# A two-layer image kernel: depthwise taps moved from TensorE to VectorE, half of one layer's statistics to ScalarE

## The chip, the cores and the metric

The kernel runs on one core of one Trainium2 chip, in one launch for the whole batch. The time is the device time of that core in microseconds (us). A core has these engines: TensorE (PE in the profile, with its weight loads as PEld) for matrix products, VectorE (DVE), ScalarE (ACT), GpSimd (POOL), and SyncE (SP), which here issues all transfers. Each engine works through its own instruction stream in order, and they meet at semaphores.

## The reference

Eight images of 128 channels and 64 x 64 pixels pass two layers. What is computed, cut to its core:

```
# layer 0
ll, lh, hl, hh = haar(x)                       # 4 bands of 32 x 32
q, k, v = conv1x1(ll, qkv_w)                   # 8 heads of 16, 1024 tokens
attn = l2norm(q) @ l2norm(k).T * 0.25          # keep the 512 largest of each row
ll_out = group_norm(conv1x1(softmax(top_half(attn)) @ v, proj_w))
y = depthwise_3x3(concat(lh, hl, hh), dw_w)    # 384 channels, 9 taps
y = group_norm(conv1x1(silu(group_norm(y)), pw_w))
x = x + 0.1 * inverse_haar(ll + ll_out, bands + alpha * y)
y = gelu(group_norm(conv1x1(x, w1)))           # 128 -> 256 channels
x = x + 0.1 * group_norm(conv1x1(y, w2))
# layer 1
q, k, v = 16, 16 and 128 channels of x, 4096 tokens
x = gamma * conv1x1(softmax(q @ k.T / 4) @ v, Wo) + x
```

A group norm needs the mean and variance of each group over all pixels before its scale is known.

## The kernel before

The images go through a pipeline of two kinds of stretches. `slots(b)` runs the attention of image b's layer 0 and, interleaved with it, that of image b - 1's layer 1. `between(f, n)` lies between two such stretches: it finishes layer 0 of image f (projection, group norms, feed-forward layers, planes of q, k and v for layer 1) and opens image n (bands, depthwise convolution, pointwise products, q, k, v of layer 0). The program is between, slots for image 0 alone, seven times between and slots for two images, and between and slots for the last image's layer 1. Six of the seven are one loop body.

Within each stretch every engine has a list written out by hand, one call per piece of work. A call waits for its semaphores and issues its instructions, so the order of the calls is the order on the engine. In `slots`, `search(h)` is the list for one of seven steps per image: the top-half threshold of head h, the row maxima of the next chunk of layer 1 (`maxima`, matmul into one PSUM bank and reduction from it), the masked weights of the previous head (`half_m`), and the norm of a chunk.

The pieces of `between` that matter here, with the lines of their instructions:

- `taps(k, t)` on DVE: tap t of the depthwise convolution of block k of 128 channels, a multiply (L2451) or multiply-add (L2454) of 128 x 1024 into `Y`. The padded bands `PAD` come from POOL. Blocks 1 and 2 have nine taps each here.
- `conv(0, h, row)` on PE (L1090): block 0, as matmuls with diagonal weights (`diag`), nine per half of the image, into PSUM; ACT copies the halves to `Y`. Each float32 matmul is two PE instructions in the profile.
- `conv(k, h)` on DVE (L2467): statistics of a half block. `moments`, `variance`, `scales` (L2335 to L2362) are the small steps of a group norm, with a sum over groups on PE (L968), a power on POOL (L2625) and a spreading on PE (L979).
- `heads_out`, `proj`, `add0` (L2318, L955, L2324, L2370): product of the heads, projection and its statistics, and the four additions that make `X1`, the input of the feed-forward layer. `squares` on PE (L1050) sums the squares of q and k; `clamp` and `norms` on DVE (from L2408) follow it, `spread` on PE (L1079) and `normal` on DVE (L2429) apply the result.
- `ffn1(k)`, k = 0 to 15: matmul (PE, L990) into one of four PSUM banks, eviction (ACT, L1479) and BN_STATS (DVE, L2377). PE may be three evictions ahead. Then `gelu` (ACT, L1487), `ffn2` (L1000, L1493, L2384), `points` (pointwise products, L1105, L2477, L1584), `norm2` and `add2` (L1500, L2392), and `values1` (L1023, L1522).

## Time and profile before

| | before |
|---|---|
| median of 3 runs | 5553.13 us (5548.35 to 5555.53) |
| the profiled execution's own time | 5553.66 us |
| its span, first to last instruction | 5551.9 us |
| mean granted TensorE clock | 0.917 |
| PE, DVE, ACT, POOL busy | 86, 83, 77, 5% |
| longest part of the chain that ended last | DVE 37%, PE 31%, issue 19%, ACT 7% |

Busy time is the time in which an engine has an instruction at work. The chain that ended last is followed back from the last instruction, at each step to what released it. A row of a timeline has the start, the time, engine, line, operation, output and input, the number of instructions merged into it and, in brackets, how long the engine had waited and for what. The granted clock is TensorE's: 1.0 is 2.4 GHz and 0.5 is 1.2 GHz.

### The profile page before, as it was taken

Reading aid. Unit: us, or ns where it says so; the run is one execution under the profiler, and the core shown is the slowest. Engines: PE = TensorE matmul, PEld = TensorE weight load, DVE = VectorE, ACT = ScalarE, POOL = GpSimd, SP = SyncE. Lnnn points to the kernel's source line nnn. Section 1 sums busy time; section 2 is a strip of 40 time slices with the busy share of each in tenths; the row PEclk is TensorE's granted clock in tenths of the full one; section 3 lists DMA queues with packets and bytes.
Section 4 is the critical chain, followed back from the end, with each engine's and each line's share of the span. In section 5 each row is a group of like instructions: output and inputs, shape, how many; then the busy total and the mean of one; then the engine's idle time right before and its main releaser. Section 6 shows DMA issues by size and latency. Waiting matters only on the chain.

```text
span 5551.9 us, 93420 instructions
## 1 busy us (share of the span) xinstructions
PE 4778.7 (86%) x30180; PEld 3098.8 (56%) x30180; DVE 4622.0 (83%) x9087; ACT 4261.9 (77%) x6779; POOL 261.5 (5%) x125
## 2 busy tenths in 40 slices
PE   4444899988999889988999889998899989997899
PEld 2000366654666456664666546665566636665588
DVE  4887789987999789987899879998799979996553
ACT  3884699948998599966999589984999769995333
POOL 2001000020000200010000100002000100000000
PEclk7555899998999989998999989999899989998899
DMA  1001200012001110012000120011200120001100
GB/s 58 8 10 52 62 15 16 13 60 64 16 21 44 38 53 18 16 61 63 15 16 13 60 64 16 17 47 35 55 16 18 55 69 15 16 13 44 35 12 16
DMA packets 103270, 185.34 MB, mean 33 GB/s; under 512 B 48536, under 2 KB 53560, under 8 KB 98008
## 3 DMA queue, kind: packets, MB, share of 16 engines
q1 hardware_dynamic: 102744, 178.93, 10.5%
q8 instruction: 256, 4.19, 0.3%
q14 instruction: 270, 2.21, 0.1%
HBM read 107.99 MB, written 67.37 MB: 32 GB/s over the span
## 4 chain that ended last, share of the span: by engine, by line
DVE 37%; PE 31%; issue 19%; ACT 7%; SPq 2%; DMA 1%; POOL 1%; DVEq 1%; ACTq 0%; POOLq 0%
PE PS L621 12%; DVE M L1798 8%; DVE MX L1966 7%; DVE work L1789 5%; PE PS L587 4%; PE PS L561 3%; ACT work L1216 3%; DVE work L1781 3%; DVE arena L1895 3%; PE PS L605 3%; PE PS L551 2%; PE PS L483 2%; ACT work L1271 1%; PE PS L1090 1%; PE PS L633 1%
## 5 line engine op out<-in xcount | busy, mean ns | idle before, releaser
L621 PEld LDWEIGHTS PS<-V,work 128*128 128x128 f32 x16384 | 2112.1, 193 | 164.6 <-ACT work L1281 23.1
L621 PE MATMUL PS<-V,work 128*128 128x129 f32 x16384 | 2130.1, 277 | 13.7 <-ACT work L1281 12.4
L1216 ACT ACTIVATE work<-arena,T 128x1024 bf16<-128x1024 f32 x1504 | 1714.9, 1145 | 23.4 <-DVE T L1709 13.1
L1966 DVE TENSOR_REDUCE MX<-PS 128x1 f32<-128x512 f32 x2048 | 1394.9, 686 | 249.9 <-PE PS L587 235.4
L1281 ACT ACTIVATE work<-PS 128x1024 f32<-128x1024 f32 x1024 | 1041.6, 1019 | 319.1 <-PE PS L605 317.2
L587 PE MATMUL PS<-KP,QP 96*128 96x512 bf16 x2048 | 844.0, 413 | 71.7 <-DVE MX L1966 32.8
L1798 DVE MAX8 M<-work 128x8 f32<-128x512 f32 x1024 | 651.2, 680 | 0.5
L605 PE MATMUL PS<-QP,KP 99*128 99x512 bf16 x2048 | 624.0, 387 | 23.2 <-ACT work L1281 19.8
L1208 ACT ACTIVATE arena<-PS 128x1024 f32<-128x1024 f32 x512 | 524.0, 1023 | 147.0 <-PE PS L483 138.5
L1895 DVE SCALAR_TENSOR_TENSOR arena<-PS,work 128x512 f32<-128x512 f32 x896 | 600.9, 683 | 33.7 <-ACT work L1271 24.3
L1271 ACT ACTIVATE work<-PS 128x512 f32<-128x512 f32 x896 | 513.8, 591 | 116.0 <-PE PS L551 112.8
L587 PEld LDWEIGHTS PS<-KP,QP 96*128 96x128 bf16 x2048 | 200.7, 98 | 502.2 <-DVE MX L1966 411.8
L483 PE MATMUL PS<-work 96*128 96x512 bf16 x1024 | 349.5, 427 | 98.5 <-ACT arena L1208 98.5
L551 PE MATMUL PS<-work 99*128 99x512 bf16 x896 | 332.5, 384 | 80.4 <-DVE arena L1895 60.4
L1781 DVE TENSOR_SCALAR work<-arena,T 128x1024 f32<-128x1024 f32 x512 | 371.4, 747 | 4.4 <-DMA scrL<-work 2.7
L1789 DVE TENSOR_SCALAR work<-work,FL 128x1024 uint32<-128x1024 uint32 x512 | 374.2, 744 | 1.0
L561 PE MATMUL PS<-arena,VT 128*17 128x256 f32 x4096 | 345.4, 415 | 3.4 <-DVE arena L1887 3.3
L1216 ACT ACTIVATION_READ_ACCUMULATOR work<-arena,T 128x1 f32 x1504 | 295.4, 196 | 0.0
L605 PEld LDWEIGHTS PS<-QP,KP 99*128 99x128 bf16 x2048 | 182.0, 99 | 185.4 <-ACT work L1281 81.2
L483 PEld LDWEIGHTS PS<-work 96*128 96x128 bf16 x1024 | 80.0, 102 | 263.6 <-ACT arena L1208 171.4
L551 PEld LDWEIGHTS PS<-work 99*128 99x128 bf16 x896 | 83.1, 98 | 198.7 <-DVE arena L1895 164.1
L2645 POOL TENSOR_TENSOR work<-work 128x1024 f32<-128x1024 f32 x8 | 22.6, 2826 | 3494.1 <-DMA work<-in_x 3494.1
(193 smaller groups left out, 4157.7 us busy)
## 6 DMA issues: line engine op xcount, KB each, us to landing
work<-scr SPq DMA_DIRECT2D x752, 32.0 KB, 1.8
work<-in_x SPq DMA_DIRECT2D x16, 1024.0 KB, 7.4
arena<-in_x SPq DMA_DIRECT2D x8, 2048.0 KB, 11.2
scrX<-arena SPq DMA_DIRECT2D x8, 2048.0 KB, 6.4
XR<-scrX SPq DMA_DIRECT2D x64, 256.0 KB, 2.7
out<-YO SPq DMA_DIRECT2D x64, 256.0 KB, 2.0
scr<-work SPq DMA_DIRECT2D x24, 512.0 KB, 2.7
scrL<-work SPq DMA_DIRECT2D x24, 512.0 KB, 7.9
```

Of the source, the lines that this page charges most:

```text
L483: last = mm(PS[:, c, :], qp(h)[0:KS, 128 * i:128 * i + 128], kp(h)[0:KS, 512 * c:512 * c + 512], start=True, stop=True)
L587: mm(PS[:, maxbank(c, k, l0), :], QP1[0:KS, c * 512 + 128 * i:c * 512 + 128 * i + 128], KP1[0:KS, 512 * w:512 * w + 512], start=True, stop ...
L605: last = mm(PS[:, pairbanks(k, l0) + t, :], KP1[0:KA, 128 * mt:128 * mt + 128], QP1[0:KA, j * 512:j * 512 + 512], start=True, stop=True)
L621: last = mm(PS[:, 5 + i // 2, 136 * (i % 2):136 * (i % 2) + 129], P1[:, (16 * j + k) % 3, t, 128 * i:128 * i + 128], V1[:, mt, :], start=( ...
L1216: A(junk[:, m % 2, :], scores(h, i), ACT.Sign, scale=-1.0, bias=T[:, h % 2, i:i + 1], accum_out=CA[:, h % 2, i:i + 1]).then_inc(s["ca"], 1)
L1271: A(JA[:, mt % 2, 512 * c:512 * c + 512], PS[:, c, :], ACT.Exp, scale=0.25).then_inc(s["e" if c else "eh"], 1)
L1281: A(P1[:, (16 * j + k) % 3, :, :].rearrange("p t n -> p (t n)"), PS[:, u:u + 2, :].rearrange("p a n -> p (a n)"), ACT.Exp, scale=0.25).the ...
L1781: cp.did(V.tensor_scalar(JD[:, c, :], scores(h, i), T[:, h % 2, i:i + 1], None, ALU.subtract))
L1789: cp.did(V.tensor_scalar(JDu[:, c, :], JDu[:, c, :], FL[:, h % 2, i:i + 1].bitcast(u32), None, ALU.bitwise_xor))
L1798: cp.did(V.max(M8[:, i, a, :], JD[:, c, 512 * a:512 * a + 512]))
L1895: V.scalar_tensor_tensor(scores(h, mt)[:, 512 * c:512 * c + 512], PS[:, c, :], 0.0, JA[:, mt % 2, 512 * c:512 * c + 512], ALU.is_ge, ALU.m ...
L1966: V.reduce_max(MX[:, c % 2, i, w:w + 1], PS[:, maxbank(c, k, l0), :], AX.X).then_inc(s["mr"], 1)
```

## The change

The convolution on PE goes: `NPE`, `diag` and the POOL instruction that filled it, `conv` on PE and the copies of it on ACT. DVE does all 27 taps. In exchange the statistics of the first eight of ffn1's sixteen pieces leave DVE: ACT sums each piece while it evicts it (`accum_out` into `FS`), and two new instructions `power1(o)` square 2048 columns each and sum them into `FQ`; their output goes to `V1`, which `values1` overwrites later. `moments(3)` puts the sums together. All lists are written anew, those between images most, and those of the search, the opening and the closing as well.

```diff
-NPE = 1
-        diag = sb("diag", [128, 9 * NPE, 128])
+        FS, FQ = sb("FS", [128, 8]), sb("FQ", [128, 2])
...
@@ ACT, between @@
-                    A(HF[:, o, 512 * ch:512 * ch + 512], PS[:, k % 4, :], ACT.Copy).then_inc(s["hc"], 1)
+                    A(HF[:, o, 512 * ch:512 * ch + 512], PS[:, k % 4, :], ACT.Copy, **({} if o else {"accum_out": FS[:, ch:ch + 1]})).then_inc(s["hc"], 1)
+
+                def power1(o):
+                    if not fin:
+                        return
+                    act.wait_ge(s["hc"], f * 16 + 4 * o + 4)
+                    act.wait_ge(s["pv1"], f * 128 + 3)
+                    A(V1[:, 16 * o:16 * o + 16, 0:128], HF[:, 0, 2 * N0 * o:2 * N0 * o + 2 * N0].rearrange("p (a c) -> p a c", c=128), ACT.Square, accum_out=FQ[:, o:o + 1])\
+                        .then_inc(s["fq"], 1)
...
+                    if k == 0:
+                        act.wait_ge(s["fq"], (f + 1) * 2)
...
-                def conv(k, h):
-                    if not opn:
-                        return
-                    if k == 0 and h == 0:
-                        act.wait_ge(s["pad"], (n + 1) * 3)
-                    act.wait_ge(s["cv"], n * (2 * NPE) + 2 * k + h + 1)
-                    act.wait_ge(s["bc"], n * 6 + 2 * k + h + 1)
-                    A(Y[:, k, 512 * h:512 * h + 512], PS[:, 5 + h, :], ACT.Copy).then_inc(s["ye"], 1)
...
+                power1(0)
                 ffn1(10)
...
                 ffn1(15)
-                values0(1)
+                power1(1)
                 gelu(0)
...
@@ DVE, moments @@
-                    w = {0: 2, 1: 2, 2: 2, 3: 8, 4: 8}[g]
+                    if g == 3:
+                        dve.wait_ge(s["fq"], (f + 1) * 2)
+                        dve.wait_ge(s["hc"], f * 16 + 8)
+                        ch.link(V.tensor_reduce(N.mv[:, 0, 0:1], FS[:, :], AX.X, ALU.add))
+                        ch.link(V.tensor_tensor(N.mv[:, 0, 1:2], FQ[:, 0:1], FQ[:, 1:2], ALU.add))
+                        ch.wait(mark["bn"])
+                        ch.link(V.bn_aggr(N.mv[:, 1, :], N.bn[:, 8:16, :].rearrange("p a s -> p (a s)")))
+                        ch.link(V.tensor_scalar(N.st[:, 0, :], N.mv[:, 0, :], 1.0 / N1, None, ALU.mult))
+                        ch.link(V.tensor_tensor(N.st[:, 1, 1:2], N.mv[:, 1, 0:1], N.mv[:, 1, 0:1], ALU.mult))
+                        ch.link(V.tensor_tensor(N.st[:, 1, 1:2], N.st[:, 1, 1:2], N.mv[:, 1, 1:2], ALU.add))
+                        V.tensor_copy(N.st[:, 1, 0:1], N.mv[:, 1, 0:1]).then_inc(s[N.sem + "1"], 1)
+                        return
+                    w = {0: 2, 1: 2, 2: 2, 4: 8}[g]
...
-                    V.bn_stats(BH[:, 2 * k + h, :], PS[:, 5 + h, :] if k < NPE else Y[:, k, 512 * h:512 * h + 512]).then_inc(s["bc"], 1)
+                    V.bn_stats(BH[:, 2 * k + h, :], Y[:, k, 512 * h:512 * h + 512]).then_inc(s["bc"], 1)
...
@@ DVE, list of between @@
+                taps(0, 0)
                 taps(2, 0)
-                taps(1, 0)
                 taps(2, 1)
```

What the lists make of the order is seen at three places. The first is DVE at the front of a stretch between two images: L2451 and L2454 (L2435 and L2438 after) are the taps, L2318 (L2290) is the product of the heads, BN_STATS of `BN<-PS` the projection's statistics. Before:

```order
L2451 TENSOR_SCALAR work<-PAD,w_dw 128x1024 x2
L2454 SCALAR_TENSOR_TENSOR work<-PAD,w_dw,work 128x1024 x4
L2317 REGISTER_ALU
L2318 TENSOR_TENSOR arena<-arena 128x1024
L2454 SCALAR_TENSOR_TENSOR work<-PAD,w_dw,work 128x1024
L2323 ISA
L2324 BN_STATS BN<-PS 128x6
```

The same place in the changed kernel:

```order
L2435 TENSOR_SCALAR work<-PAD,w_dw 128x1024 x2
L2438 SCALAR_TENSOR_TENSOR work<-PAD,w_dw,work 128x1024 x4
L2435 TENSOR_SCALAR work<-PAD,w_dw 128x1024
L2289 REGISTER_ALU
L2290 TENSOR_TENSOR arena<-arena 128x1024
L2438 SCALAR_TENSOR_TENSOR work<-PAD,w_dw,work 128x1024 x3
L2295 ISA
L2296 BN_STATS BN<-PS 128x6
```

One tap more stands ahead of the product, and three instead of one stand between it and the statistics.

The second is PE around ffn1 (L990, L987 after). L1050 (L1047) are the squares, L1090 the convolution. Before:

```order
L979 MATMUL PS<-GG,indT 128x2
L1046 REGISTER_ALU
L1050 MATMUL PS<-cons,work 128x8 x16
L1090 MATMUL PS<-PAD,diag 128x512 x3
L990 MATMUL PS<-arena,w 128x512 x4
```

After, there, and behind it the end of ffn1 with the spreads (L1076), the group sum (L965) and its spreading (L976):

```order
L976 MATMUL PS<-GG,indT 128x2
L1043 REGISTER_ALU
L1047 MATMUL PS<-cons,work 128x8 x16
L987 MATMUL PS<-arena,w 128x512 x4
...
L1076 MATMUL PS<-cons,work 128x128 x4
L986 REGISTER_ALU
L987 MATMUL PS<-arena,w 128x512
L986 REGISTER_ALU
L987 MATMUL PS<-arena,w 128x512
L1076 MATMUL PS<-cons,work 128x128 x4
```

Ffn1 stands directly behind the squares now, and a spread stands ahead of its last two matmuls.

The third is DVE in a step of the search, behind the threshold: L1966 (L1938) are row maxima, L1739 (L1711) an update of the search, L1948 (L1920) `head_out`. Before:

```order
L1966 TENSOR_REDUCE MX<-PS 128x1
L1723 REGISTER_ALU
L1739 SCALAR_TENSOR_TENSOR T<-CA,T 128x4
L1965 REGISTER_ALU
L1966 TENSOR_REDUCE MX<-PS 128x1
L1965 REGISTER_ALU
L1966 TENSOR_REDUCE MX<-PS 128x1
L1948 COPY OT<-PS 128x256
```

After:

```order
L1938 TENSOR_REDUCE MX<-PS 128x1
L1695 REGISTER_ALU
L1711 SCALAR_TENSOR_TENSOR T<-CA,T 128x4
L1920 COPY OT<-PS 128x256
L1937 REGISTER_ALU
L1938 TENSOR_REDUCE MX<-PS 128x1
L1937 REGISTER_ALU
L1938 TENSOR_REDUCE MX<-PS 128x1
```

The copy of the head's output has moved ahead of two row maxima.

## Rows read from the trace of the kernel before

**Rows 1.** The page's first part, the whole span.

```profile
PE 4778.7 (86%) x30180; PEld 3098.8 (56%) x30180; DVE 4622.0 (83%) x9087; ACT 4261.9 (77%) x6779; POOL 261.5 (5%) x125
```

**Rows 2.** Windows: us, busy us of each engine, clock, DMA; stretch between images, search step.

```profile
1197.00:1307.50 110.50, 98.37 (x364) 52.27 (x364) 77.08 (x149) 67.43 (x98) 8.22 (x7) 0.95 0.16 40
...
1510.47:1573.70 63.23, 59.44 (x430) 41.45 (x429) 58.95 (x123) 59.15 (x99) 0.00 (x0) 1.00 0.06 17
```

**Rows 3.** Timeline of DVE, image 2, front of the stretch.

```profile
1200.24 1.42 DVE L2451 TENSOR_SCALAR work<-PAD,w_dw 128x1024 f32<-128x1024 f32 x2 [4.19 <-issue]
1201.57 4.99 DVE L2454 SCALAR_TENSOR_TENSOR work<-PAD,w_dw,work 128x1024 f32<-128x1024 f32 x4
1206.48 1.22 DVE L2318 TENSOR_TENSOR arena<-arena 128x1024 f32<-128x1024 f32 x1
...
1209.44 0.70 DVE L2324 BATCH_NORM_STATS2 BN<-PS 128x6 f32<-128x512 f32 x1 [0.55 <-PE PS L955]
...
1215.60 0.16 DVE L2362 TENSOR_TENSOR SH<-vecs,SM 128x1 f32<-128x1 f32 x1
...
1220.75 1.22 DVE L2370 TENSOR_TENSOR arena<-arena 128x1024 f32<-128x1024 f32 x1
```

**Rows 4.** Timeline of PE, image 2.

```profile
1215.11 4.70 PE L1050 MATMUL PS<-cons,work 128*128 128x8 f32 x32
1219.66 5.21 PE L1090 MATMUL PS<-PAD,diag 128*128 128x512 f32 x6
1224.71 8.75 PE L990 MATMUL PS<-arena,w 128*128 128x512 f32 x20
...
1266.69 10.57 PE L1105 MATMUL PS<-work,w_pw 128*128 128x512 f32 x24 [0.22 <-ACT work L1575]
```

**Rows 5.** Windows, image 2 (columns as above; granted clock third from last).

```profile
1215.00:1220.00 5.00, 5.00 (x35) 4.99 (x35) 4.53 (x7) 1.20 (x1) 0.00 (x0) 0.77 0.00 0
1220.00:1225.00 5.00, 5.00 (x7) 2.01 (x7) 4.66 (x14) 0.00 (x0) 0.00 (x0) 0.55 0.00 0
...
1245.00:1250.00 5.00, 3.96 (x17) 2.41 (x17) 3.82 (x7) 2.63 (x3) 1.09 (x1) 1.00 0.00 0
```

**Rows 6.** Timeline of PE, last image.

```profile
5101.72 15.83 PE L990 MATMUL PS<-arena,w 128*128 128x512 f32 x32 [6.54 <-DVE arena L2370]
...
5125.52 15.87 PE L1000 MATMUL PS<-arena,w 128*128 128x512 f32 x32 [3.05 <-ACT arena L1487]
```

**Rows 7.** Timeline of DVE, first image.

```profile
51.24 0.29 DVE L2408 TENSOR_SCALAR SSM<-PS 128x128 f32<-128x128 f32 x1 [5.97 <-PE PS L1050]
...
73.47 0.35 DVE L2335 BATCH_NORM_AGGREGATE MVH<-BH 128x2 f32<-128x12 f32 x3
```

**Rows 8.** Timeline of PE, first image, and the stretch that follows it.

```profile
81.98 13.46 PE L1105 MATMUL PS<-work,w_pw 128*128 128x512 f32 x24 [2.18 <-ACT work L1575]
...
594.61 5.43 PE L1090 MATMUL PS<-PAD,diag 128*128 128x512 f32 x6
```

**Rows 9.** Timeline of ACT, image 2.

```profile
1239.54 0.60 ACT L1479 ACTIVATE arena<-PS 128x512 f32<-128x512 f32 x1 [0.26 <-PE PS L990]
...
1247.37 4.64 ACT L1487 ACTIVATE arena<-arena,SH,SC 128x1024 f32<-128x1024 f32 x4 [5.44 <-DVE SH L2362]
...
1288.82 1.02 ACT L1208 ACTIVATE arena<-PS 128x1024 f32<-128x1024 f32 x1
1289.72 0.20 ACT L1208 ACTIVATION_READ_ACCUMULATOR arena<-PS 128x1 f32 x1
```

**Rows 10.** Timeline of DVE, image 2, moments of ffn1.

```profile
1241.99 0.60 DVE L2335 BATCH_NORM_AGGREGATE MV<-BN 128x2 f32<-128x48 f32 x2
...
1243.02 0.17 DVE L2339 COPY ST<-MV 128x2 f32<-128x2 f32 x1
```

**Rows 11.** Waits of DVE in the search step: us, times, longest.

```profile
DVE MX L1966 <- PE PS L587: 2.1, 6, 0.5
DVE TP L1878 <- issue: 1.2, 1, 1.2
```

502 lines of the change are left out of this document (234 added, 268 removed).

## The prediction

> **What bounds the kernel now.** Read the page first. PE, DVE and ACT are busy for 86, 83 and 77% of 5551.9 us [rows 1], so no engine alone bounds the whole. Busy time by stretch comes next: in one step of the search (63.23 us, seven such per image) DVE and ACT work 59 us and PE 59.4 us, and in one stretch between images (1197.0 to 1307.5) PE works 98.4 of 110.5 us while DVE works 77.1 and ACT 67.4 [rows 2]. The change adds work to the two engines with room in that stretch and takes 20 us of PE's busy time from it, some of it clocked low, so the question is which of the 98.4 us the end of the stretch waits for. The timelines of DVE, PE and ACT over the stretch answer that. The chain is: heads ready, projection, its statistics, four additions that make X1, the sixteen matmuls of the first feed-forward layer (ffn1), their statistics, gelu, ffn2, the pointwise products, normalization, key and value planes of layer 1. The convolution on PE is in that chain only where its matmuls stand in PE's queue ahead of something ready.
>
> **The change, part by part.** I follow image 2, the others repeat it within a few tenths of a us in the stretches I opened.
>
> *Front, up to X1.* DVE begins its taps at 1200.24, and two first taps take 1.42 us, four later ones 4.99, so 0.7 and 1.2 us each [rows 3]. Before, six taps precede the product of the heads at 1206.48, now seven: +0.7. Behind it stood one tap and then 0.55 us of idle time before the projection's statistics at 1209.44; now stand three taps (3.6 us): 1208.35 + 3.6 = 1211.95, some 2.5 us later than before. Then come two statistics (1.25), moments (0.75), a tap (1.2), variance (0.65), a tap (1.2) that covers PE and POOL, and the scales (0.65): 1217.65 instead of 1215.76 [rows 3], as PE's convolution no longer delays the spreading of the sums. With 1.35 on ACT and four additions of 1.17 the last X1 comes at 1223.7 instead of 1221.97 (1220.75 + 1.22). That is +1.75.
>
> *What the convolution cost there.* X1 was whole at 1221.97, but ffn1 began at 1224.71, because the second half of the convolution ran from 1219.66 for 5.21 us [rows 4]. It now begins at 1223.75: a gain of 0.95, no more.
>
> *The clock.* Those six instructions took 5.21 us, while six of the same shape take 2.64 at the rate of the pointwise products (24 in 10.57) [rows 4]. The granted clock tells why: 0.77 in 1215 to 1220 and 0.55 in 1220 to 1225, where 0.5 is 1.2 GHz and 1.0 is 2.4 GHz [rows 5]. It fell during the 32 narrow instructions of the squares and rose only during the convolution, so the convolution took the slow stretch upon itself and ffn1 ran at 2.4 GHz (20 instructions in 8.75 us, 0.43 each). Without it PE stands nearly idle from 1210 to 1217, runs the squares and idles some 2 us more. ffn1 then starts at 1.2 GHz. The last image, which has no convolution, shows the price: its 32 instructions of ffn1 take 15.83 us against 13.8 at 0.43 each, so 2.0 [rows 6]. The bounds are 0 (clock still high) and 2.9, from the first image's pointwise products: 24 instructions in 13.46 us against 10.57 in image 2 [rows 4, 8]. I take 2.0, from the same matmuls. In the Trainium skill, "TensorE: Matmul & The Clock Gate", sections on the clock gate and its oscillation, the low clock is the default, activity releases it, and a burst of matmuls behind an idle gap starts slow. By that rule the removed matmuls were useful as activity, which speaks against the change. The trace agrees, with 0.55 turning into 1.00 just as the convolution ends; without this effect the stretch would keep its old clock and the third rival below would hold.
>
> *Statistics on ACT.* Eight of sixteen BN_STATS leave DVE (0.6 us each, 4.9 us), nine taps come (10.2 us), so DVE gains 5.3 us of work. It has room until ffn1, as the taps fill the time in which it waited. ACT gets eight accumulator reads (0.2 us each; they fit the 0.26 us that it waits between evictions [rows 9]) and two Squares of 128 x 2048. No instruction of 2048 columns is in the trace. Gelu of 1024 columns takes 1.16 us (four in 4.64) and an eviction of 512 columns 0.60 [rows 9], so 2048 cost at most 2 x 1.16 = 2.3 and at least 1.16 + 0.84 = 2.0, if each further 512 columns cost the 0.42 by which an eviction of 1024 (1.02) exceeds one of 512 [rows 9]; with the read I take 2.3 (2.2 to 2.5). The first Square stands behind ffn1's tenth eviction, where the four PSUM buffers and one spread matmul group hide it. The second stands behind the sixteenth and has no cover, for moments(3) waits on it. From the last eviction's end to the finished moments it was 3.1 us (1240.1 to 1243.19, DVE beginning its moments at 1241.99 [rows 9, 10]). Now it is 2.3 for the Square and 1.5 for seven small DVE instructions (0.2 each): 3.8, so +0.7. Behind the waiting moments are queued normal(1), the taps and the scales of gelu.
>
> *PE's order.* spread(0) now stands ahead of the last two ffn1 matmul groups: +1.0. Sum to gelu: -0.95 + 2.0 + 1.0 + 0.7 = +2.75.
>
> *ffn2 and the pointwise products.* PE ran these back to back, and the products began at 1266.69 [rows 4]. In the gap between ffn1 and ffn2, which grows to about 11 us with two spreads in it, the clock falls: it did so even before, in image 1, where six convolution instructions at 594.61 took 5.43 us [rows 8], and the last image's ffn2 took 15.87 against 13.97, so 1.9 [rows 6]. Taking 1.9 (0 to 2.9), and 0 for group(1), whose moments DVE has near 1262 (gelu's scales at 1250, then five taps, six statistics, a product, moments: 12 us) while PE comes to it near 1263.5 (start 1253, four times 1.75, a spread, the slow start): the products start 4.65 late. DVE's new order takes moments(4) ahead of the products' second statistics, -1.0. One eviction now stands on ACT between the normalizations, which set the pace of the last additions, +0.5, and the one of points(2,0) inside ACT's full tail up to the value planes +0.3. Stretch: +4.4 us, seven times: +31.
>
> *First and last image.* At the start DVE sat idle 5.97 us until 51.24 for the squares [rows 7]. Eighteen taps now stand ahead of clamp, which comes at 55.1, and nine of 27 remain: the high bands' moments move from 73.5 [rows 7] to 76 (35.1 + 30.7 of taps + 3.9 for clamp and norms + 2.0 of products + 3.9 of statistics + 0.5 of waits), +2.5. In the last image no tap exists; the Squares cost 0.8 of lag, and 1.8 where DVE was nearly abreast: +2.6.
>
> *The lists of the search.* All lists are rewritten here too. A step has 3.3 us of DVE waits: 2.1 for PE's row maxima, in six places, and 1.2 for the register load [rows 11]. The maxima share one PSUM bank, so two in a row on DVE wait 0.4 to 0.5 for a round trip. The new order puts head_out ahead of maxima 15 (which waited 0.41) and two flips instead of one ahead of maxima 0 (0.39), but puts maxima 29 directly behind the tiny excess pair, and leaves 15/16 and 17/18 in pairs. Net -0.3 per step. Bounds: -2.1, all waits gone, and +1.0, which is five new back-to-back pairs less what they replace; PE and ACT have under 4 us of room each, so a delay on either shows. 49 steps at -0.3: -15. The opening without layer 1 and the closing steps I put at 0 (plus or minus 6).
>
> **Sum.** 31 + 2.5 + 2.6 - 15 = +21 on the profiled execution's 5553.66 (span 5551.9 and 1.8 around it): 5574.8. The median is 0.5 below that execution: 5574.
>
> **The rivals.** *The search lists win more.* If 0.9 us of the 2.1 goes per step, 49 x 0.9 = 44 against 36 of the rest: 5545, and at most 5487 if all waits go. For it: the waits named are short and each can be filled. Against: PE is as full as DVE (59.4 of 63.23), and a filled wait on one is paid on the other. *The search lists lose:* +0.5 per step, one more round trip: 36 + 25 = +61, 5614. For it: several maxima now follow each other closer (28, excess, 29; both halves of masks ahead of 25). Against: the order moves most pieces by one place only. *The clock holds.* If PE stays at 2.4 GHz at both starts, the stretch loses 3.9 and gets a stall of about 0.5 at group(1): +1.0 per image, 7 + 5 - 15 = -3: 5550. For it: in 1245 to 1250 of image 2 the clock was 1.00 although PE idled for a fifth [rows 5]; against it, the squares already brought it down. *No effect of the edit:* excluded, since 288 matmul instructions go and 72 taps come; but a sum near zero is the case just told. *A faster result through less PE work as such* would need the convolution's 20 us in the chain; only 2.7 us of it is there.
>
> **Chances.** Forecast 0.45, with its own range 5560 to 5590; search lists lose 0.17; clock holds 0.18; search lists win more 0.20. What repeats of this kernel can tell from no change is 0.2%, 11 us. Slower by more: nearly all of the first two, 0.60. Within: half of the clock case and the edges, 0.22. Faster: the better lists and a bit of the clock case, 0.18. The range that holds 8 of 10 runs from 5538 to 5606, leaving out the ends of both list cases.
>
> **What would show it.** In the new profile of an image: X1's last addition about 1.7 us later against the first tap; the first ffn1 matmuls at 0.85 us per instruction instead of 0.43 and a granted clock near 0.5 there; again at ffn2; a Square of 2.1 to 2.3 us directly ahead of moments(3), with DVE idle before it; gelu about 2.8 us and the pointwise products 4 to 5 us later; a stretch of 115 instead of 110.5 us; a step of the search at 62.9 instead of 63.2. The forecast is wrong if ffn1 starts at full clock, if the step differs by over 0.5 us from 63.2 either way, or if the first Square makes PE wait for PSUM.

## The result and the profile after

The changed kernel takes 5624.85 us (median of 4 runs, 5623.88 to 5635.42) against 5553.76 for the kernel before beside it: a ratio of 1.0132 with an interval of 1.0120 to 1.0145. It is slower, as forecast, but by 71 us where 21 were forecast, and outside the range. The page begins:

```profile
span 5622.1 us, 92914 instructions
...
PE 4734.7 (84%) x29892; PEld 3103.1 (55%) x29892; DVE 4679.0 (83%) x9111; ACT 4279.0 (76%) x6859; POOL 261.7 (5%) x124
```

TensorE is busy 44 us less than in [rows 1], VectorE 57 us more, and the span is 70.2 us longer, so busy time doesn't say where the loss is. I cut the span at marks on VectorE: the instruction that converts the number found (FOUNDI) marks a head of the search as found, 64 of them in all. Sums in us, from the two timelines:

| | before | changed | difference |
|---|---|---|---|
| start to first head found | 166.9 | 172.7 | +5.9 |
| image 0, the other heads | 338.0 | 335.3 | -2.7 |
| seven times: last head to the next image's first | 1500.7 | 1512.9 | +12.2 |
| 7 x 7 search steps | 3039.7 | 3091.8 | +52.1 |
| last head to the end | 506.6 | 509.3 | +2.7 |

The search steps, which the forecast had at -15, are three quarters of the loss. The stretch between images is the smaller part, but only in this table: from VectorE's first tap to the first row maxima it is 3.7 us longer in the mean, 26 us in seven images, while the way from the last head to the first tap is 1.5 us shorter and that from the first row maxima to the first head 0.5 us, 14 us in seven. Cut at VectorE's first tap, the end of X1, the first of gelu's scales and the first of the silus', image 2 reads before and after (windows: us, then busy us of PE, PEld, DVE, ACT and POOL, the granted clock, DMA share, GB/s):

```profile
1200.24:1221.97 21.73, 20.29 (x74) 11.82 (x73) 18.89 (x29) 5.45 (x9) 0.54 (x1) 0.89 0.02 6
1221.97:1246.94 24.97, 23.24 (x75) 11.95 (x74) 20.79 (x43) 11.32 (x18) 3.41 (x2) 0.95 0.00 1
1246.94:1262.14 15.20, 15.20 (x52) 7.44 (x52) 13.06 (x26) 13.56 (x17) 0.54 (x1) 1.00 0.00 0
```

```profile
1213.23:1238.25 25.02, 17.77 (x54) 11.96 (x54) 22.93 (x32) 6.49 (x10) 1.52 (x1) 0.57 0.02 6
1238.25:1264.02 25.77, 20.99 (x67) 11.31 (x68) 23.78 (x43) 15.29 (x30) 3.52 (x2) 0.83 0.00 0
1264.02:1279.68 15.66, 14.52 (x49) 7.88 (x49) 14.10 (x29) 11.78 (x13) 0.54 (x1) 0.80 0.01 1
```

In each part the clock is lower and VectorE fuller. Both could be the reason, and the experiments had to separate them. Now the search (the same view of the changed kernel: a step of image 2 that is nearly as long as in [rows 2], a long one, and 2 us pieces around the long one's beginning):

```profile
1388.16:1451.47 63.31, 59.30 (x430) 41.28 (x428) 58.76 (x121) 58.89 (x99) 0.00 (x0) 1.00 0.06 16
1514.84:1579.90 65.06, 60.74 (x430) 42.79 (x429) 59.15 (x123) 59.09 (x99) 0.00 (x0) 0.97 0.06 17
```

```profile
1516.00:1518.00 2.00, 0.86 (x6) 0.43 (x5) 1.70 (x7) 1.23 (x4) 0.00 (x0) 1.00 0.02 4
1518.00:1520.00 2.00, 1.65 (x11) 1.18 (x9) 1.45 (x3) 2.00 (x5) 0.00 (x0) 0.84 0.01 2
1520.00:1522.00 2.00, 2.00 (x10) 1.84 (x10) 0.69 (x1) 1.83 (x3) 0.00 (x0) 0.50 0.03 2
1522.00:1524.00 2.00, 2.00 (x14) 1.61 (x14) 0.69 (x1) 0.61 (x2) 0.00 (x0) 0.81 0.09 18
```

Before, the 42 steps between the first and seventh head of the seven images take 62.9 to 63.5 us. Now 23 take 64.4 to 65.1 and the others 63.1 to 63.5, and the seventh step of each image, in the closing list, went from 55.2 to 56.5. In 22 of the 23 the granted clock has one dip to 0.5 that lasts 3.4 us and begins 4 to 5 us behind the found head. In the kernel before no step has one. TensorE's timeline there (turn is L526, the row maxima L586, scores and weights of layer 1 L604 and L620):

```profile
1515.21 1.06 PE L620 MATMUL PS<-V,work 128*128 128x129 f32 x8
1517.00 0.23 PE L526 MATMUL PS<-identb,TP 128*24 128x128 bf16 x1 [0.74 <-DVE TP L1853]
1517.63 0.39 PE L586 MATMUL PS<-KP,QP 96*128 96x512 bf16 x1 [0.40 <-DVE MX L1938]
1517.85 0.60 PE L604 MATMUL PS<-QP,KP 99*128 99x512 bf16 x2
1518.80 0.39 PE L586 MATMUL PS<-KP,QP 96*128 96x512 bf16 x1 [0.35 <-DVE MX L1938]
1519.03 1.60 PE L620 MATMUL PS<-V,work 128*128 128x129 f32 x8
1520.43 0.63 PE L586 MATMUL PS<-KP,QP 96*128 96x512 bf16 x1
1520.85 1.93 PE L620 MATMUL PS<-V,work 128*128 128x129 f32 x8
```

Three short waits stand around the turn (0.74, 0.40, 0.35 us), then the eight instructions that took 1.06 us take 1.60 and 1.93. The waits alone don't tell which step gets a dip: in the step at 1388.16 above, which has none, they are 0.78, 0.40 and 0.35. The kernel before waits longer once (1.42 us for the turn) and has no dip:

```profile
1558.63 0.38 PE L587 MATMUL PS<-KP,QP 96*128 96x512 bf16 x1
1560.44 0.23 PE L527 MATMUL PS<-identb,TP 128*24 128x128 bf16 x1 [1.42 <-DVE TP L1881]
1560.60 0.61 PE L605 MATMUL PS<-QP,KP 99*128 99x512 bf16 x2
1561.06 0.39 PE L587 MATMUL PS<-KP,QP 96*128 96x512 bf16 x1
1561.29 1.06 PE L621 MATMUL PS<-V,work 128*128 128x129 f32 x8
```

### The profile page after: what moved, and what is told of

The parts are those of the page before. It is cut to its first block and busy times, and to the rows that moved or that the text cites. A ratio compares the mean times of both kernels' runs of the same rounds, so it can differ in the third digit from the quotient of the medians.

```text
span 5622.1 us, 92914 instructions
## 1 busy us (share of the span) xinstructions
PE 4734.7 (84%) x29892; PEld 3103.1 (55%) x29892; DVE 4679.0 (83%) x9111; ACT 4279.0 (76%) x6859; POOL 261.7 (5%) x124
## 5 line engine op out<-in xcount | busy, mean ns | idle before, releaser
L620 PEld LDWEIGHTS PS<-V,work 128*128 128x128 f32 x16384 | 2113.5, 194 | 168.2 <-issue 34.9
L620 PE MATMUL PS<-V,work 128*128 128x129 f32 x16384 | 2140.2, 278 | 5.2 <-ACT work L1255 3.9
L1938 DVE TENSOR_REDUCE MX<-PS 128x1 f32<-128x512 f32 x2048 | 1394.2, 685 | 259.5 <-PE PS L586 241.7
L586 PE MATMUL PS<-KP,QP 96*128 96x512 bf16 x2048 | 849.3, 416 | 122.6 <-DVE MX L1938 86.8
L604 PE MATMUL PS<-QP,KP 99*128 99x512 bf16 x2048 | 620.0, 384 | 39.2 <-ACT work L1255 32.9
L586 PEld LDWEIGHTS PS<-KP,QP 96*128 96x128 bf16 x2048 | 201.6, 98 | 557.4 <-DVE MX L1938 466.1
L550 PE MATMUL PS<-work 99*128 99x512 bf16 x896 | 319.7, 385 | 41.0 <-DVE arena L1867 32.6
L560 PE MATMUL PS<-arena,VT 128*17 128x256 f32 x4096 | 319.0, 411 | 1.1 <-DVE arena L1859 1.1
L1190 ACT ACTIVATION_READ_ACCUMULATOR work<-arena,T 128x1 f32 x1504 | 309.9, 206 | 0.0
L604 PEld LDWEIGHTS PS<-QP,KP 99*128 99x128 bf16 x2048 | 176.1, 98 | 204.5 <-ACT work L1255 113.9
L2438 DVE SCALAR_TENSOR_TENSOR work<-PAD,w_dw,work 128x1024 f32<-128x1024 f32 x192 | 250.8, 1345 | 3.1 <-DVE RN L2404 1.3
L2627 POOL TENSOR_TENSOR work<-work 128x1024 f32<-128x1024 f32 x8 | 22.6, 2828 | 3565.0 <-DMA work<-in_x 3565.0
## 6 DMA issues: line engine op xcount, KB each, us to landing
arena<-in_x SPq DMA_DIRECT2D x8, 2048.0 KB, 10.2
```

What stands on the lines that cost most here:

```text
L586: mm(PS[:, maxbank(c, k, l0), :], QP1[0:KS, c * 512 + 128 * i:c * 512 + 128 * i + 128], KP1[0:KS, 512 * w:512 * w + 512], start=True, stop ...
L604: last = mm(PS[:, pairbanks(k, l0) + t, :], KP1[0:KA, 128 * mt:128 * mt + 128], QP1[0:KA, j * 512:j * 512 + 512], start=True, stop=True)
L620: last = mm(PS[:, 5 + i // 2, 136 * (i % 2):136 * (i % 2) + 129], P1[:, (16 * j + k) % 3, t, 128 * i:128 * i + 128], V1[:, mt, :], start=( ...
L1190: A(junk[:, m % 2, :], scores(h, i), ACT.Sign, scale=-1.0, bias=T[:, h % 2, i:i + 1], accum_out=CA[:, h % 2, i:i + 1]).then_inc(s["ca"], 1)
L1938: V.reduce_max(MX[:, c % 2, i, w:w + 1], PS[:, maxbank(c, k, l0), :], AX.X).then_inc(s["mr"], 1)
```

## The experiments

Each group ran beside the kernel before on its chip, which took 5551.8, 5550.9, 5553.9, 5552.4 and 5548.7 us in the five groups. It differs by 5 us between them, so differences of that size between kernels of different groups say little by themselves.

### Which part of the change costs

Two kernels split the change: one has the new stretches between images and all the old attention lists, the other the new attention lists and everything else as before. The edit exchanges the whole function on three engines:

```diff
 # both on PE, ACT, DVE
-def slots(b, l0, l1): ...   # lists of the changed kernel
+def slots(b, l0, l1): ...   # lists of the kernel before (and the other way round)
```

> The changed kernel with all lists of the stretches `slots` (search, opening, closing, image 0 alone; on TensorE, ScalarE and VectorE) put back to those of the kernel before, so that only the stretches between images are changed. The changed kernel is 70.2 us longer by its span. Adding up the stretches of the two traces I get +32.0 for the seven stretches between two images, +4.0 for the last image's, about +6 for image 0's and +28.6 for the seven stretches of searches. Theory (two separate costs that add): this kernel takes 5554 + 42 = 5596 us, its search steps are back at 63.2 us each and the granted clock in them at 1.00. Rival (the long steps follow from how the stretch between images ends, not from the search's own lists): steps of 65 us remain and the time stays near 5624.

> The kernel before with all lists of the stretches `slots` as the changed kernel has them; the convolution on TensorE, the statistics and the stretches between images are as before. Theory: 5554 + 28 = 5582 us, with about half of the search steps at 65 us and a dip of the granted clock in each of those behind the threshold, and stretches between images of the old length. Rival (the new search lists cost nothing by themselves): 5554, within 10 us.

Measured: 5584.2 us (ratio 1.0038 to 1.0071) and 5578.1 (1.0031 to 1.0065). By the marks, the first has +7.4 at the start, -1.4 in image 0, +23.9 for seven times last head to next head, 0.0 in the steps and +3.1 at the end. The second has -1.8, -2.0, -8.2, +35.0 and -1.5. Both parts cost, so both rivals fall; the first costs 32 us where 42 were expected. They sum to +54.5 of the 70.2: the rest is in the steps (+52.1 instead of +35.0), since alone the new lists have 11 dips and with the new stretches 22.

The second kernel's -8.2 came from lists too. A third one has the new closing, image-0 and opening lists on the kernel before, with the old search:

> The kernel before with the new lists only of the closing, of image 0's attention and of the opening of layer 1's row maxima; the search's list and the stretches between images are as before. In the run with all new attention lists, from the last head found to the next one found was 8.2 us less over seven images, image 0's heads and the opening 3.8 less and the end 1.5 less, while the steps cost 35 more, of which 7 x 1.3 in the last step, which belongs to both. Theory (the search's list is all of the loss): 5552 - 8 - 5 = 5539, or 5548 if the last step's 9 come from the closing. Rival (the gains there were borrowed from the search's steps): 5552.

It takes 5545.7 us (0.9979 to 0.9998), the best of all kernels here, if only by 0.1%. Its 42 search steps have their old length, its seven last steps are 1.45 us longer each, and last head to next head is 5.9 us less in all. So the search's own list carries what the 42 steps lost and the closing list what the last one lost. The gains at the ends aren't borrowed from the 42 steps, but the closing list pays 10.2 us in the last step for the 5.9 behind it. By the marks of the one traced execution, the slowest of the ten (5556.3 us), this kernel is 2.6 us longer than the kernel before, so its small gain stands on the medians alone.

### What makes a step long

Two kernels put one place of the search back, on TensorE and on VectorE:

```diff
 # PE, search: TensorE's order around the turn as before
-found_sum, l1_score(8), maxima(13), l1_weigh(7, 0), maxima(14), l1_weigh(7, 1), turn, maxima(15), l1_score(9)
+l1_weigh(7, 0), found_sum, maxima(13), l1_weigh(7, 1), l1_score(8), maxima(14), turn, l1_score(9), maxima(15)
 # DVE, search, the other kernel
-head_out, maxima(15), maxima(16)
+maxima(15), maxima(16), head_out
```

> The changed kernel with one place of TensorE's search list put back to the order before: from found_sum to the second row maxima behind turn (l1_score(8) again behind l1_weigh(7), and l1_score(9) directly behind turn, ahead of maxima 15). Theory (TensorE has too little ready work around the threshold in the new order, its granted clock falls to 0.5 for 3.4 us there and each such step is 1.7 us longer): no dip, steps at 63.2 to 63.4, so 23 long steps x 1.7 = 39 us less than the changed kernel, 5586. Rival A (what makes the step long is VectorE's head_out ahead of maxima 15, which holds back TensorE's bank): dips and 5624 remain. Rival B (the position is a symptom: the whole new list is longer): steps stay at 65 without a dip.

> The changed kernel with one call of VectorE's search list put back: head_out again behind maxima 15 and 16 instead of ahead of them. Theory that TensorE's order at the turn is the cause: 5624 within 6 us, dips remain. Rival (head_out, 0.4 us, ahead of maxima 15 delays the release of the maxima's bank so that TensorE stands idle): the dips go and the time is near 5586.

The first takes 5677.2 us: my theory in this form is wrong. There are still 21 dips, and a step without one now takes 64.3 to 64.5 us (one 65.6), 1.0 more than in the changed kernel. The trace tells why the dips stay: with only this place put back, TensorE doesn't wait once for 1.42 us as in the kernel before, but for 1.30 and 0.79:

```profile
1399.81 0.23 PE L526 MATMUL PS<-identb,TP 128*24 128x128 bf16 x1 [1.30 <-DVE TP L1853]
...
1401.61 0.45 PE L586 MATMUL PS<-KP,QP 96*128 96x512 bf16 x1 [0.79 <-DVE MX L1938]
1401.86 1.93 PE L620 MATMUL PS<-V,work 128*128 128x129 f32 x8
```

So the edit left TensorE idler around the turn (2.1 us against 1.5 in the changed kernel), and didn't test what it was meant to. One engine's list can't be put back at one place without the others'. The second takes 5623.5, as long as the changed kernel, with 18 long steps and the same three waits: head_out isn't the cause.

Next, work for TensorE instead of another order: four matmuls that nobody reads (bf16, 512 columns), once around the turn, once 4 us behind it, once 19 us ahead of it.

```diff
+def filler(bank, k):
+    for _ in range(k): mm(PS[:, bank, :], KP1[0:KS, 0:128], KP1[0:KS, 0:512], start=True, stop=True)
 # e5: l1_weigh(7, 1), filler(1, 2), turn, filler(0, 1), maxima(15), l1_score(9), filler(0, 1), maxima(16)
 # e6: l1_weigh(8, 1), filler(0, 4), maxima(18)
 # e18: inside score(h, 5), ahead of its products, filler(0, 4)
```

> The changed kernel with four more matmuls per search step on TensorE whose results nobody reads (bf16, 512 columns, 0.22 us each): two ahead of turn, one ahead of maxima 15 and one ahead of maxima 16, where TensorE otherwise idles 0.74, 0.40 and 0.35 us. 23 of its 42 steps took 64.9 to 65.1 us and had 3.4 us at the low clock behind the threshold, the others 63.4 without. Theory (TensorE's thin activity there brings the clock down): all steps 63.4, 23 x 1.6 = 37 us less, 5588. Rival (the dips depend on when in the program's time a step falls, whatever stands there): some 15 to 25 steps stay long, about 5624. Second rival (the added work delays what waits): all steps longer, over 5640.

> The control: the same four matmuls per search step, but all of them behind l1_weigh(8), ahead of maxima 18, some 4 us after the turn. Theory of thin activity at the turn: dips stay, steps 65 plus up to 0.9 for the added work, 5624 to 5660. Rival (any 0.9 us of TensorE work per step keeps the clock up): like the run with the filled turn, 5588.

> The changed kernel with the four unread matmuls of the two filled runs placed ahead of the scores of score(h, 5), some 19 us before the turn, where TensorE is busy without a gap. Theory (what counts is TensorE's activity near the turn): the number of long steps stays near 23 (18 to 24), steps up to 0.9 longer for the work, 5624 + up to 38: 5630 to 5662. Rival (any added work, or the shift of the steps in time, removes the dips): seven or fewer long steps.

| | us | dips | step without a dip |
|---|---|---|---|
| changed kernel | 5624.9 | 22 | 63.1 to 63.5 |
| filled at the turn (e5) | 5593.9 | 0 | 63.1 to 63.6 |
| filled 4 us later (e6) | 5647.1 | 7 | 63.9 to 64.4 |
| filled 19 us ahead (e18) | 5652.8 | 12 | 63.9 to 64.4 |

Around the turn the four matmuls are free and remove every dip (one step in image 3 took 64.8 without one; the changed kernel has such a step too, the 23rd), and the steps fall from 3091.8 to 3059.0 us: 33 us for 22 dips, 1.5 each. Elsewhere the same work lengthens every step by its 0.8 us and dips remain, in each kernel 4 to 5 us behind a found head. There are fewer of them than I expected, though: not each thin turn gets a dip, and shifting the steps in time changes which do. That the shift alone removed them in the filled kernel is unlikely: all five other kernels with the new search list whose steps are shifted, each in its own way (the two fillers elsewhere, the two with one place put back, the one with only the new attention lists), keep 7 to 21. TensorE in the filled kernel, with its window below (waits of 0.30 us for the turn and 0.13 behind it are left of 1.5):

```profile
1574.62 0.23 PE L526 MATMUL PS<-identb,TP 128*24 128x128 bf16 x1 [0.30 <-DVE TP L1860]
1574.77 0.39 PE L675 MATMUL PS<-KP 96*128 96x512 bf16 x1
1575.24 0.39 PE L586 MATMUL PS<-KP,QP 96*128 96x512 bf16 x1
...
1576.64 1.06 PE L620 MATMUL PS<-V,work 128*128 128x129 f32 x8
```

```profile
1573.00:1579.00 6.00, 5.49 (x36) 3.69 (x36) 3.85 (x11) 5.23 (x10) 0.00 (x0) 1.00 0.01 3
```

### Clock or VectorE in the stretch between images

These kernels start from the one with only the stretches changed (5584.2 us), where no search step has a dip. The table gives means over seven images in us, between ends on VectorE: first tap to X1, X1 to gelu's scales, these to the first statistics of the pointwise products, these to the last addition, that to the first row maxima; then how long the last image takes from its last head to its first row maxima.

| | us | tap to X1 | X1 to gelu | to products | to additions | to maxima | sum | last image |
|---|---|---|---|---|---|---|---|---|
| before | 5553.8 | 23.2 | 24.6 | 23.0 | 16.1 | 23.5 | 110.4 | 127.4 |
| changed | 5624.9 | 24.9 | 25.8 | 25.1 | 15.7 | 22.6 | 114.1 | 130.7 |
| only stretches changed (e1) | 5584.2 | 25.4 | 25.6 | 25.3 | 15.7 | 22.6 | 114.6 | 130.7 |
| dead convolution (e7) | 5587.3 | 25.0 | 26.3 | 24.6 | 15.7 | 22.7 | 114.2 | 129.2 |
| front filled (e8) | 5590.3 | 25.3 | 25.4 | 25.2 | 15.7 | 22.7 | 114.3 | 133.9 |
| filled up to ffn1 (e12) | 5587.4 | 24.9 | 25.3 | 25.4 | 15.7 | 22.6 | 113.9 | 130.8 |
| gap to ffn2 filled (e9) | 5589.5 | 25.1 | 25.8 | 23.5 | 15.7 | 23.3 | 113.5 | 126.6 |
| heads early (e11) | 5610.1 | 24.5 | 28.7 | 25.4 | 15.7 | 22.5 | 116.9 | 130.4 |
| heads early, filled (e19) | 5613.9 | 23.8 | 28.8 | 26.0 | 15.7 | 22.6 | 116.8 | 132.5 |
| statistics on DVE (e13) | 5607.5 | 24.9 | 28.0 | 25.5 | 15.7 | 22.6 | 116.7 | 126.4 |
| less ahead of moments (e14) | 5614.4 | 25.3 | 25.4 | 29.1 | 15.7 | 22.8 | 118.2 | 130.6 |

*TensorE's idle time filled.*

```diff
 # e7: the old convolution matmuls at their old places, identity as weights, unread
+conv(0, 0, 0) ... conv(0, 1, 2)
 # filler(k): k unread matmuls of 384 columns, f32
 # e8:  qk0(0), filler(3), values0(0), qk0(1), filler(4), ..., filler(2), group(0), filler(5), ungroup(0)
 # e12: e8, and squares(), filler(4), ffn1(0)
 # e9:  ffn1(15), spread(1), filler(4), group(3), filler(3), ungroup(3), filler(2), spread(2)
```

> The kernel with only the stretches between images changed (5584 us), and on TensorE the eighteen convolution matmuls of each image put back at their old places, with the identity as weights and nobody reading their result: the activity without the use. Theory (the convolution's work kept TensorE's clock up: heads' projection at 1.88 instead of 3.49 us, squares at 4.70 instead of 7.00, ffn1 at full clock): X1 about 3 us earlier, ffn1 at 0.43 per instruction, stretch 3 us shorter, 7 x 3 = 21 less: 5563. Rival (the longer stretch comes from VectorE's nine more taps and its order): as before this edit or longer by up to the 2.7 us per image of convolution ahead of ffn1: 5584 to 5603.

> The kernel with only the stretches between images changed (5584 us), with fourteen unread matmuls of 384 columns on TensorE, all ahead of the squares, where it stood waiting: three behind qk0(0), four behind qk0(1), two ahead of group(0), five ahead of ungroup(0). Theory (clock): projection and squares at 2.4 GHz, X1 3 us earlier and ffn1 at 0.43 us per instruction (2.0 us), 4 to 5 us less per stretch, 7 x 4.5 = 31: 5553. Rival (VectorE's order sets X1): X1 where it was, at most the 2.0 of ffn1, 5570; if the fillers only delay, over 5584.

> The run with the front filled (5590 us; squares at full clock, end 3 us ahead of X1, ffn1 still at the low clock: 14 instructions in 8.30 us) with four more unread matmuls between the squares and ffn1, in the 2.97 us in which TensorE waited for X1. Theory (the low clock at ffn1 costs 2 us and is the only cost of the clock there): ffn1's first fourteen instructions in 6.1 us, 7 x 2 = 14 less than 5590: 5576. Rival (the rest of the chain to gelu, values0 and spread on TensorE and evictions and Square on ScalarE, takes up what ffn1 gains): over 5585.

> The kernel with only the stretches between images changed (5584 us), with nine unread matmuls of 384 columns on TensorE in the gap between ffn1 and ffn2: four ahead of group(3), three ahead of ungroup(3), two behind it. There the clock was 0.50 from 1256 to 1262 and the first twelve instructions of ffn2 took 6.93 us instead of 5.42. Theory (clock): ffn2 starts at 2.4 GHz, the pointwise products begin 1.5 us earlier in each of seven images, ffn2 as much in the last: 8 x 1.5 = 12 less, 5572. Rival (ScalarE's gelus, evictions and silus, 20 us in a row, set the start of the products, not ffn2): 5584 within 4 us.

The dead convolution brings the mean clock back to the 0.917 of the kernel before, and the time not at all. It costs what it gives: ffn1 runs fast but begins 2.8 us behind X1 in the mean, as one of the six parts of the convolution stands ahead of it. With the front filled the squares run fast, and TensorE then waits 3 us for an X1 that comes no earlier:

```profile
1226.37 3.74 PE L1047 MATMUL PS<-cons,work 128*128 128x8 f32 x32
1233.08 8.30 PE L987 MATMUL PS<-arena,w 128*128 128x512 f32 x14 [2.97 <-DVE arena L2362]
```

The kernel filled up to ffn1 has two kinds of images, which its mean hides. In images 2 and 3 squares and filler together took over 9.6 us (in image 2 the filler's 8 instructions of 384 columns 5.47), and ffn1, fast, began 2.7 and 2.9 us behind X1. In the other five they took at most 8.3, and ffn1 began at most 1.4 us behind X1, fast too. Taken from the end of X1, in us:

| | ffn1 begins | ffn1 ends | last eviction ends | last statistic ends | gelu's scales |
|---|---|---|---|---|---|
| changed, mean of 7 | 0.2 | 18.2 | 18.9 | 21.3 | 25.8 |
| only stretches changed, mean of 7 | 0.2 | 18.0 | 18.7 | 21.1 | 25.6 |
| filled up to ffn1, images 2 and 3 | 2.8 | 18.6 | 19.3 | 21.7 | 26.2 |
| filled up to ffn1, the other 5 | 1.0 | 16.8 | 17.4 | 20.5 | 25.0 |

In every image of the first three rows the last statistic ends 2.4 us behind the last eviction: VectorE follows TensorE there. In the five images of the last row it ends at 20.5, whether the eviction ends at 16.7 or at 17.7: that is VectorE's own queue, now without a wait. The two images of the dead convolution's kernel in which ffn1 ends at 17.0 show the same 20.5. VectorE's rows, image 2 (X1 at 1232.74) and image 4 (X1 at 2539.64) of the filled kernel:

```profile
1248.39 2.47 DVE L2370 BATCH_NORM_STATS2 BN<-arena 128x6 f32<-128x512 f32 x4 [1.13 <-ACT arena L1462]
...
2553.48 3.05 DVE L2370 BATCH_NORM_STATS2 BN<-arena 128x6 f32<-128x512 f32 x5
```

So the slow start of ffn1 isn't free: gelu comes 0.6 to 0.8 us earlier without it, some 5 us in seven images, and the rest of its 2.3 us VectorE's queue takes up. The gap to ffn2 is worth more:

```profile
1258.15 0.60 PE L976 MATMUL PS<-GG,indT 32*128 32x2 f32 x4
...
1261.81 5.42 PE L997 MATMUL PS<-arena,w 128*128 128x512 f32 x12 [0.67 <-ACT arena L1476]
```

The twelve instructions took 6.93 us without the fillers, and the products come 1.7 us earlier (25.26 to 23.54): here the clock is in the chain. The last image gains 4.1 us, 2.5 of them in ffn2 itself (16.54 to 14.00). The whole time didn't follow (5589.5), since in this kernel the stretch from the last head to the first tap is 1.3 us longer and the one behind the first maxima 0.9. These wander by such amounts from image to image in every kernel, and why they did so here stays open. In time the theory of the clock failed in all four kernels; the rivals held in three, and in the last neither did (5572 or 5584 within 4 us were expected).

*VectorE's order and load.*

```diff
 # DVE, e11: taps around the heads' product as before the change
-taps(2, 3), taps(1, 0), heads_out(), taps(2, 4), taps(1, 1), taps(0, 2), proj(0)
+taps(2, 3), heads_out(), taps(1, 0), proj(0)      # the others behind add0(3); e19: and e8's fillers
 # e13: no accum_out, no power1; norms(), ffn1(0) to ffn1(3), taps(0, 6), ffn1(4) to ffn1(7), taps(2, 6) on DVE
 # e14: taps(0, 6), taps(2, 6), taps(0, 7) behind scales(3); ACT: power1(1) behind ffn1(12)
```

> The same kernel of 5584 us, with VectorE's list at the front of the stretch put back in one respect: six taps instead of seven ahead of the heads' product and one instead of three between it and the projection's statistics; the three taps go behind the four additions, and those between the small steps move up. With TensorE's waiting time filled there (a run before this one) the projection came at full clock, yet X1 did not come earlier, so the new theory is that VectorE's taps set X1: X1 2.2 us earlier relative to the last head, 7 x 2.2 = 15 less, 5569. Rival (what is moved only shifts: clamp, norms and spread come 3.6 us later and hold back the statistics of ffn1 behind them in the queue): 5584 or more.

> The kernel with only the stretches between images changed (5584 us), with both the old order of taps ahead of and behind the heads' product (alone: X1 0.8 us earlier against the first tap) and the front filled on TensorE (alone: 0.2 to 0.5). Theory (two nearly level paths, VectorE's taps and TensorE's projection at the low clock, cover each other): X1 2.0 to 2.4 us earlier against the first tap. Rival (each is worth its own small part): 1.0 to 1.3. In both cases the three moved taps come behind X1 and gelu is as late as in the run with the order alone, so no time is won: about 5605.

> The kernel of 5584 us with the statistics of ffn1 all on VectorE again (sixteen BN_STATS, the eight of the first half behind norms, in two fours around a tap), no sums in ScalarE's evictions and no Square: of the change only the taps are left, with the new lists. Theory (VectorE is the later of the two at moments(3), so that its 4.9 us more come out nearly whole, less the 0.8 of small steps): gelu 4 us later in eight stretches: 5584 + 32 = 5616. Rival (the Square on ScalarE stood in the way and sets the moments, as my prediction had it with +0.7): 5584 within 6 us or less.

> The kernel of 5584 us (only the stretches between images changed) with three taps (3.6 us) moved on VectorE from ahead of moments(3) to behind scales(3), and on ScalarE the second Square moved from behind the sixteenth eviction of ffn1 to behind the thirteenth. In that kernel VectorE had no gap from X1 to moments(3) (last statistic done at 1253.6) and the Square ended at 1253.1, both after the last eviction at 1251.2. Theory (VectorE's queue bounds X1 to gelu, the Square just behind): gelu 1.7 us earlier in seven stretches and some 2 us in the last: 14 less, 5570. Rival (the time lies in TensorE's ffn1 at the low clock): 5584 within 4 us. Second rival (the three taps are then late for the silus): gelu earlier, products not.

Up to X1 the old order alone gives 0.8 us, the fillers alone 0.1 and both 1.6: two nearly level strands, which together explain most of the 2.2, a bit less than I expected. The three taps behind X1 then delay gelu by 3.1. Eight more statistics delay it by 2.4, less than the 4 expected. In both kernels the last statistic has one fixed end in all images, 24.2 and 23.6 us behind X1, instead of 21.1: 3.7 and 3.2 above VectorE's own 20.5, less the 0.6 by which VectorE was following TensorE. So from X1 to gelu added work on VectorE comes out whole, once it has used up that 0.6. Taking work away is different: with three taps less ahead of the moments VectorE waits for evictions (rows of ACT's L1453 as releaser), gelu comes only 0.2 earlier, and the same taps now hold up the silus, so that the products are 3.8 us later.

```profile
1249.77 0.69 DVE L2361 BATCH_NORM_STATS2 BN<-arena 128x6 f32<-128x512 f32 x1 [2.11 <-ACT arena L1453]
1252.80 2.47 DVE L2361 BATCH_NORM_STATS2 BN<-arena 128x6 f32<-128x512 f32 x4 [2.33 <-ACT arena L1453]
...
1256.63 1.88 DVE L2361 BATCH_NORM_STATS2 BN<-arena 128x6 f32<-128x512 f32 x3 [0.78 <-ACT arena L1453]
```

An idle moment that VectorE gets ahead of the silus is paid for: it is nine tenths busy from the first tap to their scales in the changed kernel. So of the four expectations the rival held for the old order alone, the numbers for order and fillers together fell between the two, the statistics went with the theory at two thirds of its size, and for the moved taps the second rival held.

Two sums of such edits, the second with the new ends and the last image's statistics on VectorE:

> The run before, and the gap between ffn1 and ffn2 filled on TensorE with the nine unread matmuls, and gelu(6) again ahead of the third and fourth eviction of ffn2 on ScalarE, as in the kernel before the change. Filled alone, the gap gave 1.7 us from VectorE's first tap to the last addition. Theory (gains add): 5570 - 7 x 1.7 = 5558. Rival (fillers ahead of group(3) now stand in the way, since moments(3) come earlier): 5570 or more.

> The changed kernel with the old search list, the new closing and image-0 lists, the taps and the Square moved as above, the gap to ffn2 filled, gelu(6) in its old place, and in the last image, which has no taps, the statistics of ffn1 all on VectorE without a Square (4.3 us less in the run that had it so). Sum: 5558 of the run above, less 4 for the last image, less 8 to 13 for the ends: 5541 to 5546, against 5552 of the kernel before. If the ends' gains are borrowed: 5554.

They took 5627.0 and 5613.0 us. Both contain the three moved taps, so they failed with them: from gelu's scales to the products it is 28.6 and 28.7 us, against 25.3 in the kernel with only the stretches changed. In the second the last image was 4.3 us shorter, as hoped. In the first it wasn't, though its gap to ffn2 is filled (ffn2 in 14.68 us): there X1 to gelu took 3.7 us longer, so the last image, one per run, is a weak witness.

## Why the prediction was wrong

**The step that failed** is "The lists of the search", put at -0.3 per step and -15 in all. It measured +52.1: about 10 for the new order without dips (the 42 steps of the kernel filled at the turn are 10.3 longer than before, 0.25 each, inside the bounds of -2.1 and +1.0), 9 for the last step of each image in the closing list, and 33 for the dips. I had counted waits of VectorE for its row maxima, and these are as they were, 2.2 us in six places against 2.1 [rows 11]:

```profile
DVE MX L1938 <- PE PS L586: 2.2, 6, 0.5
DVE TP L1850 <- issue: 1.2, 1, 1.2
```

The term lacked the clock, and the 9 us lay in a list that I had put at 0. Which of the moves in the search list makes the 10 stays open. In a step in which TensorE works 59 of 63 us at 1.00 [rows 2] I took the clock as given, though I had the effect in the text for the stretch between images. The rival "the search lists lose" had sign and place (+61 in all against a measured 71), with another mechanism.

**Between images** the sum was nearly right: +3.7 per image from first tap to first maxima, forecast +4.4. Its terms fared unequally. Outside these two marks, where I had nothing, the stretches won 2.0 us each, so that of the 26 us only 12.2 are left in the table of the result.
- X1: forecast +1.75, measured +1.7. But I saw the taps alone behind it. The low clock of the projection is a second, level strand.
- Ffn1 at 1.2 GHz happens as forecast (14 instructions in 8.46 us against 6.17, 0.60 each against 0.44), and spread(0) costs 0.9. With the earlier start, 2.6 us against X1, ffn1 ends 0.6 us later against X1 in image 2. But the slow start isn't worth 2.0 at gelu: 0.8 by the table of ffn1 above, since VectorE's own queue ends only so much before. X1 to gelu is +1.2 against a forecast +1.0, with TensorE and VectorE within 0.8 us of each other. I had written that VectorE "has room until ffn1" and stopped there. Behind X1 it has little: five taps, norms, two taps, the statistics, with one wait of 0.64 for the eviction behind the first Square (1250.89 to 1252.89), which I had called hidden.
- The Square: 1.90 and 0.19 for the read, below my 2.2 to 2.5 and near the lower of the two estimates from which I chose (2.0). In image 2 its read ended at 1258.93 (1258.74 + 0.19), VectorE's last statistic at 1259.45 (1258.77 + 0.68): VectorE was the later of the two by 0.5 us. From the last eviction's end to the moments' it is 3.85 us against 3.20, so the +0.7 had its size, but by luck: a tap and a statistic of VectorE make it, not the Square, and VectorE isn't idle ahead of the moments as I had said. ACT's rows, then VectorE's:

```profile
1256.44 0.60 ACT L1453 ACTIVATE arena<-PS 128x512 f32<-128x512 f32 x1 [0.26 <-PE PS L987]
1256.94 1.90 ACT L1460 ACTIVATE V<-arena 128x2048 f32<-128x2048 f32 x1
1258.74 0.19 ACT L1460 ACTIVATION_READ_ACCUMULATOR V<-arena 128x1 f32 x1
```

```profile
1253.41 2.47 DVE L2361 BATCH_NORM_STATS2 BN<-arena 128x6 f32<-128x512 f32 x4 [0.64 <-ACT arena L1453]
...
1258.77 0.68 DVE L2361 BATCH_NORM_STATS2 BN<-arena 128x6 f32<-128x512 f32 x1
```

- Ffn2 at the low clock: forecast +1.9 to the products, measured +2.1, and the filled gap gave 1.7 back. This term held, with its mechanism.
- The additions: forecast -0.5, measured -0.4. The tail up to the maxima: forecast +0.3, measured -0.9.

In "TensorE: Matmul & The Clock Gate" of the Trainium skill, section on the clock gate, activity of the array releases the high clock. The runs agree for ffn2 (twelve instructions in 5.42 us instead of 6.93 with the gap filled) and for the turn (no dip in 42 steps). What the rule doesn't say is whether the fast instruction is in the chain, and what the activity costs there: the dead convolution raised the mean clock from 0.905 to 0.917, but started ffn1 2.6 us later for the 2.0 by which it sped it up.

**The first image** lost 5.9 instead of 2.5. The high bands' moments came at 80.83 instead of the 76 that I had. Its 27 taps took 33.5 us in the timeline, not 30.7, and some 3 us of waits around clamp and spread stood where I had put 0.5:

```profile
42.10 13.36 DVE L2438 SCALAR_TENSOR_TENSOR work<-PAD,w_dw,work 128x1024 f32<-128x1024 f32 x11
56.00 0.29 DVE L2392 TENSOR_SCALAR SSM<-PS 128x128 f32<-128x128 f32 x1 [0.53 <-PE PS L1047]
...
80.83 0.35 DVE L2319 BATCH_NORM_AGGREGATE MVH<-BH 128x2 f32<-128x12 f32 x3
```

**The last image**: forecast +2.6, measured +3.3 from last head to first maxima: 1.6 less up to X1, which the kernel with only the new attention lists shows too, and 4.9 more behind it, 2.1 of them from X1 to gelu. So this term was too small for its own part. Without the Squares the image is 4.3 less, of which 1.2 lie from X1 to gelu and 0.9 in ffn2. Where VectorE has no taps, the exchange only costs, and the longer gap slows ffn2 further (16.70 us against 15.87 in [rows 6]):

```profile
5167.61 15.98 PE L987 MATMUL PS<-arena,w 128*128 128x512 f32 x32 [6.54 <-DVE arena L2354]
5193.47 16.70 PE L997 MATMUL PS<-arena,w 128*128 128x512 f32 x32 [3.04 <-ACT arena L1469]
```

**The closing lists** I had at 0 plus or minus 6: in the kernel with only the new attention lists last head to next head is 8.2 us less, and the last step takes 9 of it back, so the 0 was near.

## What to carry to other kernels

When lists are reordered in a loop that fills TensorE, look for the place in a round at which several engines wait for one small result, and read the granted clock there in 2 us pieces, in many rounds and not in one. A few unread matmuls at such a place cost nothing and may be worth more than the order of everything else. A slow clock costs time only as far as the slow instruction is in the chain, so before pricing it, follow the other strands to the same meeting point; where they are level within a microsecond, added work counts nearly in full and removed work hardly at all. And look at the images one by one: a mean of seven hid here that five gained and two lost.
